# Attention with experts on one core: the expert products in three passes, softmax stripes in six buffers, and the logits copied out of their bank

## The reference

```
q, k, v = x @ wq.T, x @ wk.T, x @ wv.T            # 16 heads of 32 features, no scale
attention = softmax(q @ k.T) @ v, heads joined, @ wo.T
logits = x @ Wr.T + br                            # 8 experts
h = x @ A (8 experts x rank 64), y = (h @ B) / 64
experts = y of the expert with the largest logit, times its softmax probability
```

## Time and profile before

| | us |
|---|---|
| median of the runs | 1540.71 |
| the profiled execution | 1541.77 |
| its span in the trace | 1540.0 |
| busy: TensorE matmuls | 1480.7 |
| busy: VectorE | 932.6 |
| busy: ScalarE | 776.8 |
| busy: GpSimd | 1159.7 |
| mean granted TensorE clock | 0.986 |

### The profile page before, as it was taken

One profiled execution on the slowest core, in us unless ns is written; L12 is line 12 of the kernel. 1 busy time (PEld: TensorE's weight loads), 2 busy tenths in 40 slices (PEclk: granted clock), 3 DMA queues, 4 the chain that ended last, 5 costly groups with the idle time before them and its releaser, 6 DMA issues.

```text
span 1540.0 us, 20530 instructions
## 1 busy us (share of the span) xinstructions
PE 1480.7 (96%) x6872; PEld 865.1 (56%) x6872; DVE 932.6 (61%) x1722; ACT 776.8 (50%) x1421; POOL 1159.7 (75%) x654
## 2 busy tenths in 40 slices
PE   7999999989999999999999999999999999999998
PEld 5755456655645656556645555556664555554354
DVE  6756667655565566665566556666556666564633
ACT  3455555544555455545546445554555545455232
POOL 0376879978798867877889987777987888888301
PEclk9999999999999999999999999999999999899999
DMA  7355624444431422427242323324514222210001
GB/s 237 92 165 150 208 80 135 142 148 131 124 77 42 117 84 61 126 80 254 52 130 64 90 70 103 104 68 153 158 39 148 49 49 63 56 42 29 1 13 42
DMA packets 80217, 153.13 MB, mean 99 GB/s; under 512 B 19041, under 2 KB 26225, under 8 KB 79729
## 3 DMA queue, kind: packets, MB, share of 16 engines
q1 hardware_dynamic: 78720, 150.24, 33.5%
q0 software_dynamic: 336, 1.07, 0.2%
q10 hardware_dynamic: 1056, 0.52, 0.1%
HBM read 102.52 MB, written 48.49 MB: 98 GB/s over the span
## 4 chain that ended last, share of the span: by engine, by line
PE 78%; issue 7%; DVE 6%; POOL 4%; DMA 3%; ACT 1%; SPq 1%; POOLq 0%; ACTq 0%; DVEq 0%
PE w L684 14%; PE pv L827 13%; PE mx L805 13%; PE sc L815 13%; PE w L750 6%; PE w L763 6%; PE w L719 5%; DVE mxc L1037 3%; PE mx L778 2%; POOL Psum L595 2%; DMA spread_s<-den_s 1%; PE mx L743 1%; PE mx L763 1%; PE w L727 1%; DMA den_parts<-spread_s 1%
## 5 line engine op out<-in xcount | busy, mean ns | idle before, releaser
L1037 DVE TENSOR_REDUCE mxc<-mx 128x1 f32<-128x512 f32 x1024 | 683.8, 686 | 463.9 <-PE mx L805 460.8
L908 ACT ACTIVATE P<-sc 128x512 f32<-128x512 f32 x1024 | 598.8, 597 | 504.8 <-PE sc L815 490.6
L595 POOL TENSOR_TENSOR Psum<-Psum,P 128x1024 f32<-128x1024 f32 x296 | 695.7, 2383 | 26.5 <-ACT P L908 24.7
L815 PE MATMUL sc<-stack 98*128 98x512 f32 x1024 | 540.4, 530 | 7.5 <-ACT P L908 6.9
L805 PE MATMUL mx<-stack 96*128 96x512 f32 x1024 | 407.1, 402 | 9.1 <-DVE mxc L1037 4.6
L815 PEld LDWEIGHTS sc<-stack 98*128 98x128 f32 x1024 | 194.3, 190 | 142.7 <-issue 81.0
L805 PEld LDWEIGHTS mx<-stack 96*128 96x128 f32 x1024 | 195.9, 191 | 124.2 <-issue 70.8
L827 PE MATMUL pv<-P,V 128*32 128x512 f32 x2048 | 250.4, 607 | 0.0
L592 POOL TENSOR_TENSOR Psum<-P 128x1024 f32<-128x1024 f32 x50 | 118.6, 2390 | 132.7 <-ACT P L908 126.4
L684 PE MATMUL w<-xT_s,wqk_s 128*128 128x512 f32 x624 | 197.9, 408 | 12.0 <-DVE xT_s L1054 10.4
L684 PEld LDWEIGHTS w<-xT_s,wqk_s 128*128 128x128 f32 x624 | 116.9, 192 | 67.7 <-issue 43.4
(11 more groups left out here) (147 smaller groups left out, 1086.8 us busy)
## 6 DMA issues: line engine op xcount, KB each, us to landing
stack<-qk_parts SPq DMA_DIRECT2D x186, 256.0 KB, 4.3
qk_parts<-split SPq DMA_DIRECT2D x56, 512.0 KB, 3.4
wqk_s<-wqk_parts SPq DMA_DIRECT2D x24, 512.0 KB, 4.5
xT_s_f<-xT SPq DMA_DIRECT2D x8, 1024.0 KB, 6.5
den_s<-den_parts SPq DMA_DIRECT2D x124, 64.0 KB, 2.1
r_f<-x SPq DMA_DIRECT2D x3, 2048.0 KB, 11.2
out<-r_f SPq DMA_DIRECT2D x12, 512.0 KB, 3.1
qk_parts<-turned SPq DMA_DIRECT2D x8, 512.0 KB, 3.9
```

Of the source, the lines that this page charges most:

```text
L595: pool.tensor_tensor(sums(s)[:, i, :], sums(s)[:, i, :], P[:, unit % NP, :], ALU.add).then_inc(add_done, 1)
L815: pe.matmul(sc[c][:, :], stack(s, i)[0:KS, 0, 128 * kb:128 * kb + 128], stack(s, i)[0:KS, 1, 512 * c:512 * c + 512], start=True, stop=True ...
L908: act.activation(P[:, unit % NP, 512 * c:512 * c + 512], sc[c][:, :], ACT.Exp).then_inc(exp_done, 1)
L1037: dve.tensor_reduce(mxc[:, q % 2, at:at + 1], BANK["max", g][:, :], AX.X, ALU.max).then_inc(mx_done, 1)
```

## The change

- `h`, `z` and `lg` become three-pass products on high and low parts: 12 matmuls each. yT and hmT get a low part: ScalarE writes the high part out of the bank, VectorE subtracts it from the bank a half later (`yT_low`, `hmT_low`), and that frees the `mx` bank. wr is split once in slot 2. A and B are loaded raw in slots 3 and 5, split by ScalarE (`ab_high`) and GpSimd (`ab_low`, 8 subtractions in slots 4 and 5), stored in DRAM, and A's parts are loaded into `wide` for each batch; B's parts stay in `wb`.
- To make room, `P` has 6 stripe buffers in place of 7, and `xT_s` holds the parts of 512 tokens in place of 1024. For batches 0 and 1 the other 512 tokens lie in `wb`. For batches 2 and 3 the second half of the tokens is split first (4 of each in slots 9 and 17), its qk pieces run, its parts are kept in DRAM (`keep_x`), the first half is loaded and split, its qk and v pieces run, and the second half's parts are loaded back (`again_x`, 2 MB) at half 0 of slots 16 and 24 for the last 4 v pieces. Filler of these two slots begins at half 8 (`FROM`).
- So each qk weight slice of batches 2 and 3 is loaded twice: one load for each piece.
- `tail(s)` holds for slots 0 to 7.
- The order of qk pieces among the experts is a list written out by hand.
- VectorE copies the logits to SBUF; ScalarE's exponentials read that copy, four halves after lg (before: one or two), the inverse of the sum follows at six (before: three). The `lg` bank is free when the winner is marked (`eq_done`).

```diff
-    NP, NMX = 7, 3
+    NP, NMX = 6, 3
...
+        b, m = divmod(n, 16)
+        if b > 1:
+            return b, m % 8 // 2, m % 2, 1 - m // 8
+        return (b, m // 4) + (FIRST_QK[m] if n < 4 else QK_OF[m % 4])
...
+    def load_of(n):
+        return SLICES + (n - 16) // 2 if n < 32 else n - 16
...
-    CHUNKS = {"qk": PASSES * KT, "v": PASSES * KT, "o": KT, "part": KT - 1, "h": KT, "z": KT, "t1": 1, "t2": 1, "lg": 1, "den": 1}
-    COST = {"qk": 13, "v": 13, "t1": 24, "t2": 24}
+    CHUNKS = {"qk": PASSES * KT, "v": PASSES * KT, "o": KT, "part": KT - 1, "h": PASSES * KT, "z": PASSES * KT, "t1": 1, "t2": 1,
+              "lg": 1, "den": 1}
+    COST = {"qk": 13, "v": 13, "h": 13, "z": 13, "t1": 24, "t2": 24}
...
+        some = (2, 2, 2, 1, 1, 0, 1, 2, 1, 1) if fill else (0,) * (KB + 2)
...
+            if not final:
+                FROM[at + PAIRS] = 8
...
+    LOAD_X, X_HIGH, X_PASS, X_LOW, KEEP_X, AGAIN_X = {}, {}, {}, {}, {}, {}
...
+            if batch == 1:
+                load, first, step = HALVES * 3 + (1, 9)[c], HALVES * 3 + 10 + 7 * c, 1
+            elif turn == 0:
+                load, first, step = HALVES * (PAIRS * (batch - 1) + 1) + 3, HALVES * (PAIRS * (batch - 1) + 1) + 11, 4
+            else:
+                load = 1 + max(half for half, done in ENDS.items() if ("qk", 16 * batch + 7) in done)
+                first, step = load + 6, 2
+            LOAD_X[load] = batch, c
...
+            if batch > 1 and turn == 0:
+                KEEP_X[place + 8] = batch
+        if batch > 1:
+            AGAIN_X[HALVES * PAIRS * batch] = batch
...
+    SPLIT_AT, WR_AT = {"a": HALVES * 4, "b": HALVES * 5 + 8}, HALVES * 2 + 20
...
-        return s < 4 or s == LAST
+        return s < PAIRS or s == LAST
...
-                    "t2": hmT_done, "lg": lexp_done, "xi": x_lo}
+                    "t2": hmT_done, "lg": eq_done, "xi": x_lo}
...
+        def x_half(b, c):
+            return (wb_f, wb) if b < 2 and c else (xT_f, xT_s)
...
+                if b > 1 and c == 0:
+                    sp.wait_ge(x_kept, 16 * (b - 1))
+                    sp.wait_ge(qk_ready, 16 * b + 8)
...
+            def keep_x(b):
+                sp.wait_ge(x_lo, 2 * KT * b + KT)
+                sp.dma_start(x_d[b - 2], xT_s[:, :, :, :].bitcast(f32)).then_inc(x_kept, 16)
+            def again_x(b):
+                sp.wait_ge(qk_ready, 16 * (b + 1))
+                sp.wait_ge(v_ready, KB * b + KB // 2)
+                sp.dma_start(xT_s[:, :, :, :].bitcast(f32), x_d[b - 2]).then_inc(x_again, 16)
...
+            def store_ab(n):
+                sp.wait_ge(ab_lo, KT * (n + 1))
+                sp.dma_start((a_d, b_d)[n].rearrange("p a k d -> p (a k) d"), r_s[:, :, :].bitcast(f32)).then_inc(ab_stored, 16)
...
+                sp.wait_ge(ab_stored, 32)
...
-                for s, d in ((a_s, aT), (b_s, bT)):
-                    sp.dma_start(s, d.rearrange("(k p) n -> p k n", p=128)).then_inc(ab_loaded, 16)
+                sp.dma_start(wide[:, :, :, :].bitcast(f32), a_d).then_inc(a_loaded, 16)
+                if b == 1:
+                    sp.wait_ge(qk_ready, 32)
+                    sp.dma_start(wb[:, :, :, :].bitcast(f32), b_d).then_inc(b_loaded, 16)
...
-                sp.wait_ge(z_ready, KB * (b - 1))
+                sp.wait_ge(h_ready, KB * (b - 1))
...
-                    if n % 2 and n >= 17 and n // 2 + 2 < SLICES * B:
-                        load_weights(n // 2 + 2)
+                    if n >= 16 and n == last_of(load_of(n)) and load_of(n) + 2 < LOADS:
+                        load_weights(load_of(n) + 2)
...
+            def ab_low(n, kt):
+                pool.wait_ge(ab_hi, KT * n + kt + 1)
+                pool.tensor_tensor(r_s[:, KT + kt, :], r[:, KT + kt, :], r_s[:, kt, :].bitcast(f32), ALU.subtract).then_inc(ab_lo, 1)
...
+                    if b > 1 and half:
+                        pe.wait_ge(x_again, 16 * (b - 1))
+                    else:
+                        pe.wait_ge(x_lo, 2 * KT * b + KT * (half + 1 if b < 2 else 2))
...
-                for kt in range(KT):
-                    done = pe.matmul(bank[:, 0:E], yT[:, 128 * kt:128 * kt + 128], wr_s[:, kt, :], start=(kt == 0), stop=(kt == KT - 1))
+                    pe.wait_ge(wr_lo, 1)
+                for c in range(PASSES * KT):
+                    kt, at = c // PASSES, slice(128 * (c // PASSES), 128 * (c // PASSES) + 128)
+                    done = one_of_three(bank[:, 0:E], [yT[:, i, at] for i in range(2)], [wr_s[:, i, kt, :] for i in range(2)], c)
...
+                    pe.wait_ge(a_loaded, 16 * min(n // KB + 1, B - 1))
+                done = one_of_three(bank[:, :], [yT[:, i, at] for i in range(2)], [wide[:, i, kt, :] for i in range(2)], c)
...
+                    pe.wait_ge(b_loaded, 16)
+                done = one_of_three(bank[:, :], [hmT[:, i, at] for i in range(2)], [wb[:, i, kt, :] for i in range(2)], c)
...
-                act.activation(yT[:, :], bank[:, :], ACT.Copy).then_inc(yT_done, 1)
+                act.activation(yT[:, 0, :], bank[:, :], ACT.Copy).then_inc(yT_hi, 1)
...
-                act.activation(hmT[:, :], bank[:, :], ACT.Copy, scale=SCALING).then_inc(hmT_done, 1)
...
+                act.activation(hmT[:, 0, :], bank[:, :], ACT.Copy, scale=SCALING).then_inc(hmT_hi, 1)
...
-                act.activation(lexp[:, :], bank[:, E:2 * E], ACT.Exp, bias=nlmax[:, :], accum_out=lsum[:, n % 2:n % 2 + 1]).then_inc(lexp_done, 1)
+                act.activation(lexp[:, :], logits[:, :], ACT.Exp, bias=nlmax[:, :], accum_out=lsum[:, n % 2:n % 2 + 1]).then_inc(lexp_done, 1)
...
-                for n in LOGITS.get(half, ()):
-                    softmax_sum(n, BANK["lg", n])
+                for n in ends(half - 4, "lg"):
+                    softmax_sum(n)
...
+            def yT_low(n, bank):
+                dve.wait_ge(yT_hi, n + 1)
+                dve.tensor_tensor(yT[:, 1, :], bank[:, :], yT[:, 0, :].bitcast(f32), ALU.subtract).then_inc(yT_done, 1)
+            def hmT_low(n, bank):
+                dve.wait_ge(hmT_hi, n + 1)
+                dve.scalar_tensor_tensor(out=hmT[:, 1, :], in0=bank[:, :], scalar=SCALING, in1=hmT[:, 0, :].bitcast(f32),
+                                         op0=ALU.mult, op1=ALU.subtract).then_inc(hmT_done, 1)
...
                     dve.wait_ge(lexp_done, n)
+                dve.tensor_copy(logits[:, :], bank[:, E:2 * E])
                 dve.tensor_reduce(nlmax[:, :], bank[:, E:2 * E], AX.X, ALU.max, negate=True).then_inc(lmax_done, 1)
                 dve.tensor_reduce(lmax[:, :], bank[:, E:2 * E], AX.X, ALU.max).then_inc(lmax_done, 1)
...
+                    elif kind == "t1":
+                        yT_low(n, bank)
...
-                for n in ends(half - 3, "lg"):
+                for n in ends(half - 6, "lg"):
...
```

More of the change, by code:

```diff
@@ L67, in expert_pieces @@
         fill = list(fill)
-        some = [len(fill) * (n + 1) // (KB + 2) - len(fill) * n // (KB + 2) for n in range(KB + 2)]
+        some = (2, 2, 2, 1, 1, 0, 1, 2, 1, 1) if fill else (0,) * (KB + 2)
         def take(n):
@@ L208, in build_attention_lora_moe_block @@
         if half in X_PASS:
-            batch, m = X_PASS[half]
-            frees = next_turn(("xi", 2 * KT * batch + m))
+            batch, turn, kt = X_PASS[half]
+            frees = next_turn(("xi", 2 * KT * batch + KT * turn + kt))
         for kind, n, _ in AT.get(half, ()):
@@ L237, in build_attention_lora_moe_block @@
                         NORM[kind, KB * batch + group[0] + m] = len(NORMS) - 1
-    LOGITS = {}
-    for half, done in ENDS.items():
-        s, h = divmod(half + 1, HALVES)
-        for kind, n in done:
-            if kind == "lg":
-                LOGITS.setdefault(half + (1 if s and h == den_at(s) else 2), []).append(n)
     def ends(half, kind):
@@ L544, in _ @@
                     load_x(*LOAD_X[half])
+                if half in KEEP_X:
+                    keep_x(KEEP_X[half])
+                if half in AGAIN_X:
+                    again_x(AGAIN_X[half])
+                for n, place in enumerate(SPLIT_AT.values()):
+                    if half == place - 8:
+                        load_raw_ab(n)
+                    if half == place + 24:
+                        store_ab(n)
                 if h == 2 and p == 1 and b + 1 == B:
@@ L653, in _ @@
                     x_low(*X_LOW[half])
+                for n, place in enumerate(SPLIT_AT.values()):
+                    if half in range(place + 4, place + 4 + 4 * KT, 4):
+                        ab_low(n, (half - place) // 4 - 1)
             for group in range(NORM["o", FIRST], len(NORMS)):
@@ L707, in v @@
                     pe.wait_ge(wv_lo, kt + 1)
-                done = one_of_three(bank, [xT_s[:, i, kt, 128 * kb:128 * kb + 128] for i in range(2)],
-                                    [wide[:, i, kt, :] for i in range(2)], c)
+                done = one_of_three(bank[:, :], [x_parts[:, i, kt, at] for i in range(2)], [wide[:, i, kt, :] for i in range(2)], c)
```

(16 more changed lines are left out.)

187 lines of the change are left out of this document (101 added, 86 removed).

## The result

The changed kernel takes **1636.88 us** (median of 4 runs, 1632.13 to 1638.05). The kernel before took 1540.87 on the same chip (1540.62 to 1546.65). The ratio is 1.0608, 95% interval 1.0575 to 1.064: 6% slower, where 1529 was forecast.

A forecast was written before the change was run, and what follows sets the result against it. TensorE was taken as the bound, busy 1480.7 of 1540 us. Terms of -30.7, +9.6, -5.5, +10, +7, +2, -6, -4 and +6 summed to -11.6, giving 1529 us; own range 1519 to 1538, overall 1507 to 1549.

The forecast's parts named there:

- The low parts on VectorE: 48 mx banks of t1 and t2 go back one 0.68 us operation later; a third cost 0.4 each: +6 us.
- Rival 2: Each of the 48 low parts delays the maximum three turns on by 0.68: 33 us, not 6; 1556 us; chance 0.18.
- the closing part: Eight tiles with nothing beside them gain 0.88 each, less two exposed low parts of 0.75: -5.5 us.
- The second half of x: Loading it back at half 0 of slots 16 and 24 costs 3.5 us a slot: +7 us, ends 2 and 14.
- Slots 4 to 8: The new tail and GpSimd's split of A and B make den wait for GpSimd: +10 us, ends 4 and 14.
- The passes: In slots 10 to 30 an h or z chunk goes from 0.86 to 0.70 us, 192 times: -30.7 us.
- the two reliefs: Half of x_low leaving slots 9/10 and 17/18, -6 us, and the lg bank coming back earlier, -4 us.
- the weights: qk weight slices loaded twice make TensorE wait in slots 15 and 23, 1 us each: +2 us, 0 to 6.
- slot 10's relief: With half of x_low gone, slot 10 loses its wait for nmr; part of the -6 us for slots 10 and 18.
- The logits' price: 12 lg matmuls of 8 columns at 0.10 take 1.21 us a tile, +0.40; over 24 tiles +9.6 us.
- rival 1: Cheap lg passes, no clock fall in slots 5 and 6, loads in time, VectorE's part hidden: 1509 us; chance 0.27.
- The `lg` bank: Freed by eq instead of ScalarE's exponential, it ends most of 6.8 us of mx waits: -4 us, 0 to -9.

The follow-up runs named there:

- e2_low_first: Changed kernel with the low parts of yT and hmT ahead of the half's additions, statistics and qk subtraction in VectorE's order: 1619.68 us.
- e3_no_low: Changed kernel without the low parts of yT and hmT (zeros, ScalarE's copy frees the bank, all three passes still run): 1563.68 us.
- e11_stand_in: e3_no_low with VectorE running statistics of a constant tile (0.69 us, no bank held) where each low part was: 1573.77 us.
- e1_wr_gpsimd: Changed kernel with the subtraction for wr's low part moved from VectorE to GpSimd, one half later: 1622.65 us.
- e5_b_later: Changed kernel with the 2 MB load of B's parts moved from slot 9's beginning to its half 20: 1626.78 us.
- e10_no_reload: e9_no_low_wr_b also without the 2 MB loads of x at slots 16 and 24, with filler there from half 0: 1535.86 us.
- e6_before_logits: Kernel before with only the logits' part of the change (SBUF copy, later exponentials and inverse, bank free at eq_done): 1537.28 us.
- e8_logits_old: Changed kernel with the logits handled as before: no copy, exponentials out of the bank, bank free after them: 1637.28 us.
- e9_no_low_wr_b: Changed kernel without yT's and hmT's low parts, with wr's low part on GpSimd and B's parts loaded at half 20: 1546.92 us.

## Why the prediction was wrong, by its own steps

**The low parts on VectorE: the step that failed.** The forecast took "a third of the 48, 0.4 each: +6", with 0 to 33 as its ends. It measured 73, some 7 of them in the closing part (its length: 104.0, without the low parts 96.7). Rival 2 had the mechanism and the sign: it asked for waits for the subtractions that sum to more than 18 us, and they are 42.5. But its 33 was no upper end either. Four things were left out of it. First, the price of a late bank isn't the operation's own 0.68 but all that VectorE has ahead of it: `add_experts` and the statistics, named in the text, make it 3.02 us in slot 11 (order: 17 us by `e2_low_first`). Second, the time until the bank is wanted was too long: "three turns later, about 3 halves" holds for t1 (20 of 24 tiles), but by the plan of the changed kernel the third turn after t2 comes two halves later for 18 tiles and one half later for three, in slots 11, 12 and 18, where the waits are 3.02, 2.40 and 2.29. Third, the bank that comes late is not only asked for by maxima; `lg` wants it too (12.9 us in six waits). Fourth, stalls bring the lower clock behind them: 31 stretches at the lower level in the changed kernel's trace, 16 in that of `e3_no_low`. The forecast priced this behind the stalls it knew, in slots 4 to 8, and not behind the ones it averaged away: 37 of the 73. "VectorE is idle 39%" argued about the engine, and `e11_stand_in` shows that the engine's time was worth 10; what was short was the time of the bank. The argument with the right unit was there: three banks, taken in turn; the forecast had t2 "behind a z" as the case that doesn't fit, and then gave it a third.

In the closing part the forecast had the first t1's low part exposed for 0.75. It stands there behind VectorE's additions and statistics of the attention, and `lg` waits 5.67 for it; in `e3_no_low` the same `lg` waits 0.78, for ScalarE's copy. So the closing part, forecast at -5.5, came out at -0.5 (104.5 before).

**wr's subtraction: not priced at all.** It is one small operation, and stood in no term. It cost 14 us by `e1_wr_gpsimd` (12.1 of them in slot 2), as it fell into a run of GpSimd's adds.

**A's and B's loads: not priced in slot 9.** The rows held the 9.8 us of a 2 MB load; that two of them and 1 MB of x stand ahead of the sums' small transfers was to be seen in SyncE's order. 10 us by `e5_b_later`.

**The second half of x: +7 forecast, 8 by the slots of the changed kernel, 11 to 12 by `e10_no_reload`**, inside its bounds of 2 to 14. The wait came where it was said, before the first v: 2.71 us where 0.5 was forecast and 1.22 where 2 was. The trace names no releaser ("issue"), but the load was issued at 800.63, and the two loads of this form take 9.9 us to land. Timeline of TensorE of the changed kernel, slots 16 and 24:

```profile
811.37 0.95 PE L751 MATMUL w<-wide,xT_s 128*128 128x512 f32 x3 [2.71 <-issue]
...
1191.98 0.94 PE L751 MATMUL w<-wide,xT_s 128*128 128x512 f32 x3 [1.22 <-issue]
```

**Slots 4 to 8: +10 forecast, about +11 measured** as a sum: +5.3, +3.1, +9.5, -7.3 and +0.7. Its parts were only half right, so that the sum came out is luck. Of the two new waits of `den` the one in slot 6 came, the one in slot 5 didn't: there the wait is for the next slot's stack, whose loads stand behind the 2 MB store of A's parts. Timeline of the changed kernel, SyncE and TensorE:

```profile
256.67 0.34 SPq L450 DMA_DIRECT2D a_parts<-r  x1
...
260.70 3.84 SPq L537 DMA_DIRECT2D stack<-mrow  x4
...
268.00 0.79 PE L894 MATMUL sc<-stack 98*128 98x512 f32 x1 [4.79 <-DMA stack<-mrow]
...
315.96 1.93 PE L858 MATMUL mx<-wo_s,ones 128*32 128x512 f32 x8 [6.14 <-POOL wo_s L657]
```

**The passes: right in length, optimistic in what they leave.** In the closing part of `e3_no_low`, where nothing else is in the way, the tiles' logits start 7.78 us apart, before 8.59. That is 0.81 a tile; 0.88 was forecast:

```profile
1502.30 1.40 PE L751 MATMUL w<-wr_s,turned 128*128 128x8 f32 x12
1510.08 1.40 PE L751 MATMUL sc<-wr_s,turned 128*128 128x8 f32 x12
```

Beside attention, slots 10 to 30 of `e10_no_reload` are 16 us shorter than before. By the forecast's terms without low parts and reload they should be 29 shorter (30.7 for the passes, 10 for the two reliefs, less 9.6 for the logits and 2 for the weights). What of the 13 missing us is named: slot 21, +4 by the wait of `den` for GpSimd, so "it does not bind" held on average and not in every slot; slot 15, +3.4, and slot 23, +1.9, by the weights, in place of 1 each; and slot 10's relief, about 4, which didn't come. Its wait for nmr is as long as ever. Timeline of ScalarE and TensorE of the changed kernel:

```profile
519.91 0.81 ACT L1041 ACTIVATE r_f<-r_f,nmr,rstd 128x512 f32<-128x512 f32 x1 [3.65 <-POOL nmr L671]
...
521.26 0.50 PE L894 MATMUL sc<-stack 98*128 98x512 f32 x1 [3.18 <-ACT P L991]
```

Slot 18's relief did come once the low parts were gone: 49.0 before, 45.9 in `e3_no_low`. Some 2 us stay unplaced, which is less than one slot can differ by between two of these kernels with the same work in it (slot 3: 40.8 to 42.9).

**The logits' price: right.** 12 matmuls of 8 columns at the full clock take 1.26 us; 1.21 was forecast. Timeline of TensorE, slot 10:

```profile
527.67 1.40 PE L751 MATMUL mx<-wr_s,turned 128*128 128x8 f32 x12
528.93 0.48 PE L894 MATMUL sc<-stack 98*128 98x512 f32 x1
```

0.105 a pass. The 62 ns that the Trainium skill gives for the sequencer where the hardware decoder is off ("TensorE: Matmul & The Clock Gate", "Part 2: What happens when you issue a matmul") are not reached in f32r either, so the part of rival 1 that hung on a cheaper pass is out.

**The `lg` bank: -4, right alone** (`e6_before_logits`), **not to be seen in company** (`e8_logits_old`). The forecast summed it with the delays of the same ring of banks; that the two don't add is likely and not shown.

**The sum, by the chain of runs.** From the changed kernel 73 us go with the low parts (`e3_no_low`), 17 with wr and B (`e9_no_low_wr_b`; by single runs 14 and 10), 11 with the reload (`e10_no_reload`). What is left of the change is, in the slots of that last kernel against the kernel before: +11 in slots 4 to 8, -16 in slots 10 to 30, -1 in slot 31, -8 in the closing part, and +6 in slots 0 to 3, slot 9 and the part ahead of slot 0; -8 together, where its span is 7.7 shorter. That kernel leaves the 64 subtractions and the two loads out, so it is a sum done by the chip and not a version to use. The change without its four unforeseen or under-priced terms does little: the passes' gain pays for slots 4 to 8 and not for much else.

What stays open: how much of the bank's share of the 63 us could be had back with a fourth `mx` bank, which would have been the direct test of the ring. It wasn't tried, as all eight banks are in use beside attention. Nor is it settled why slots 0, 1 and 3 together with the part ahead of them are 3 to 5 us longer, in kernels with and without the low parts.

## What to carry to other kernels

Price an operation that is added between a bank's writer and its release by the bank, not by its engine: take the time from write to release, with all that stands ahead of it in its engine's order, against the time until that very bank comes round again, for every user of the ring. Count the time until the bank comes round for each user by itself: here it was three halves for one and two or one for another. Where the engine that sets the time is also the one whose clock falls when it stands still, price the clock beside the stalls: here 34 us of standing still went with 37 of lost clock. Look at each small operation and each large transfer that is put into an order written out by hand for what it stands behind and in front of: here a subtraction of 32 columns cost 14 us and an early load 10.

## What the runs showed of the hardware

- A VectorE operation whose operands are all in SBUF (128x32, the subtraction of wr) took 11.19 us while GpSimd made eight adds in a row, and ended with them; VectorE's operations out of banks beside the same adds took their usual 0.69. On GpSimd the same subtraction took 0.29, and a larger one (128x512) with both operands in SBUF took VectorE 0.68 at 12 to 60 us, when GpSimd had no adds. So neither the form nor the size made it slow. The Trainium skill ("SBUF — State Buffer", "SBUF: two separate sides") has VectorE and GpSimd share a port pair that is held for a whole instruction, where VectorE has two SBUF inputs. The trace agrees that VectorE was blocked, but not for one instruction alone: four adds of GpSimd began while it waited (11.19 us against 2.33 for an add). Where GpSimd has a gap behind an add, VectorE waits for that one add alone, and GpSimd's next add waits for VectorE's. Timeline of the closing adds of slot 31, both engines with both inputs in SBUF; an add takes VectorE 1.23 by itself, and 2.18 when it has to wait for the add that ends at 1512.86:

```profile
1510.49 2.37 POOL L657 TENSOR_TENSOR wqk_s_f<-wqk_s_f,P 128x1024 f32<-128x1024 f32 x1 [2.23 <-ACT P L991]
1511.77 2.18 DVE L1197 TENSOR_TENSOR wqk_s_f<-wqk_s_f,P 128x1024 f32<-128x1024 f32 x1 [0.62 <-ACT P L991]
...
1519.86 1.23 DVE L1197 TENSOR_TENSOR wqk_s_f<-wqk_s_f,P 128x1024 f32<-128x1024 f32 x1 [1.42 <-ACT P L991]
1519.90 3.43 POOL L657 TENSOR_TENSOR wqk_s_f<-wqk_s_f,P 128x1024 f32<-128x1024 f32 x1
```

- After a stall of TensorE of 3 us the granted clock was 0.54 for 6.9 us, so that the loss was about twice the stall. Over the whole kernel 42.5 us of such stalls, in 33 waits, went with 74 more us at the lower level.
- A pass of 8 columns in f32r starts 0.105 us after the one before (12 in 1.26), one of 512 columns 0.233.
- The 2 KB transfers of the sums, issued behind 5 MB of loads, were through at 457.1, some 10 us after the last of them was issued; their median in the same kernel is 1.8 us.
